# Context attention and projections of a batch's two chunks in one pass, with q, k, v loaded once

## The reference, cut to what matters

```python
# layer 0: 16 heads of 64 over 64 context rows, bias fside added twice
qh, kh, vh = heads(x @ wq + bq), heads(ctx @ wk + bk), heads(ctx @ wv + bv)
w = softmax(qh / 8 @ kh.T + fside + fside)
x = layernorm((w @ vh) @ wo + bo + x, eps=1e-6) * ln_g + ln_b            # the outer norm
# layer 1, 16 heads of 32
h1 = layernorm(x, eps=1e-5) * ln1_g + ln1_b                              # the inner norm
x = attention(h1, h1, quantised q, k, v, weights) @ wo + bo + x          # over all 1024 rows of the batch
h2 = layernorm(x) ...; x = attention(h2, ctx) @ wo + bo + x
h3 = layernorm(x) ...; a, g = split(h3 @ ff_w1 + b1)
x = (a * gelu(g)) @ ff_w2 + b2 + x
```

## Time and profile before

| | |
|---|---|
| median of 3 runs | 3404.15 us (3402.14 to 3405.04) |
| profiled execution, span | 3406.4 us |
| TensorE busy | 2956.5 us, 87% |
| VectorE / ScalarE / GpSimd busy | 2099.8 / 1669.4 / 1772.2 us |
| stage A of batch 0, from the first transpose of x | 120.5 to 376.8 us |
| stage A of batches 1, 2, 3 | 913.3 to 1161.4, 1695.2 to 1944.3, 2477.3 to 2728.3 us |

### The profile page before, as it was taken

The page is one execution under the profiler, slowest core; times in us unless marked ns, Lnnn a source line. Parts: engine busy times, 40 slices in busy tenths (PEclk is TensorE's granted clock), DMA queues, the critical chain, the costliest instruction groups (busy, mean ns, idle before and its releaser), DMA issues.

```text
span 3406.4 us, 50798 instructions
## 1 busy us (share of the span) xinstructions
PE 2956.5 (87%) x19712; PEld 2148.8 (63%) x19712; DVE 2099.8 (62%) x3031; ACT 1669.4 (49%) x2690; POOL 1772.2 (52%) x1695
## 2 busy tenths in 40 slices
PE   7677686887899899799889899899988889889999
PEld 6555455556677657566667656656777646656777
DVE  4556585773666586685565586676565577677521
ACT  5332572873333475574333375475333276386321
POOL 3554573884545274575355185475365176376321
PEclk9888657898999899899999999899999989999999
DMA  8753103334443213324353313323353322232444
GB/s 276 220 200 133 56 1 133 108 119 179 162 164 141 91 63 125 130 88 155 130 176 111 123 51 141 126 74 135 133 188 99 142 75 100 97 120 75 171 152 160
DMA packets 199758, 436.40 MB, mean 128 GB/s; under 512 B 94944, under 2 KB 103392, under 8 KB 182368
## 3 DMA queue, kind: packets, MB, share of 16 engines
q1 hardware_dynamic: 199520, 433.15, 36.1%
HBM read 363.38 MB, written 65.54 MB: 126 GB/s over the span
## 4 chain that ended last, share of the span: by engine, by line
PE 60%; DVE 11%; POOL 11%; ACT 7%; issue 6%; DMA 2%; SPq 1%; POOLq 0%; DVEq 0%; ACTq 0%
PE psum L1724 17%; PE psum L1726 15%; PE psum L1725 15%; PE psum L2020 5%; POOL w1b L998 3%; PE psum L2008 3%; DVE mx L1612 2%; ACT e L1302 2%; PE psum L2034 2%; ACT psum L1189 1%; DVE w1T L1624 1%; POOL u_lo L1017 1%; POOL rec L993 1%; DMA fw_lo<-pieces 1%; POOL w_lo L901 1%
## 5 line engine op out<-in xcount | busy, mean ns | idle before, releaser
L1612 DVE TENSOR_REDUCE mx<-psum 128x1 f32<-128x1024 f32 x512 | 623.1, 1218 | 121.2 <-PE psum L2009 121.0
L998 POOL TENSOR_SCALAR w1b<-e,rec 128x1024 f16<-128x1024 f32 x512 | 574.7, 1122 | 138.6 <-PE psum L2020 66.3
L1302 ACT ACTIVATE e<-psum,nb,scale 128x1024 f32<-128x1024 f32 x512 | 617.5, 1206 | 19.8 <-POOL w1b L998 3.1
L1724 PE MATMUL psum<-h_hi,fw_hi 128*128 128x512 f32 x1024 | 464.9, 454 | 30.9 <-DVE h_lo L1388 10.0
L1624 DVE TENSOR_SCALAR w1T<-psum 128x1024 bf16<-128x1024 f16 x512 | 352.0, 687 | 176.4 <-PE psum L2020 163.6
L1725 PE MATMUL psum<-h_lo,fw_hi 128*128 128x512 f32 x1024 | 415.8, 406 | 0.0
L1726 PE MATMUL psum<-h_hi,fw_lo 128*128 128x512 f32 x1024 | 415.2, 405 | 0.0
L2020 PEld LDWEIGHTS psum<-ident,w1b 128*128 128x128 f16 x4096 | 260.7, 105 | 207.7 <-issue 127.7
L2020 PE MATMUL psum<-ident,w1b 128*128 128x128 f16 x4096 | 354.3, 236 | 40.2 <-DVE w1T L1624 21.1
L907 POOL TENSOR_TENSOR rstd<-ve,mhalf 128x1 f32<-128x1 f32 x128 | 86.8, 678 | 484.8 <-DVE ve L1494 484.8
L1724 PEld LDWEIGHTS psum<-h_hi,fw_hi 128*128 128x128 f32 x1024 | 199.6, 195 | 152.4 <-issue 99.4
(11 more groups left out here) (181 smaller groups left out, 6237.0 us busy)
## 6 DMA issues: line engine op xcount, KB each, us to landing
fw_hi<-pieces SPq DMA_DIRECT2D x168, 512.0 KB, 3.3
fw_lo<-pieces SPq DMA_DIRECT2D x168, 512.0 KB, 4.4
w_hi<-kept SPq DMA_DIRECT2D x45, 1024.0 KB, 4.9
w_lo<-kept SPq DMA_DIRECT2D x45, 1024.0 KB, 7.4
mixed<-mixed SPq DMA_DIRECT2D x32, 1024.0 KB, 5.4
fbias<-in_fside_Bx16xSxS SPq DMA_DIRECT2D x64, 256.0 KB, 3.2
unsplit<-in_L_xattn_ff_w SPq DMA_DIRECT2D x24, 512.0 KB, 5.1
pieces<-fw_hi SPq DMA_DIRECT2D x24, 512.0 KB, 2.7
```

Source lines behind the costliest of these rows:

```text
L998: pool.tensor_scalar(w1b[u % NH][:], e1[u % NE][:], rec1[:, u % 8:u % 8 + 1], HALF, ALU.mult, ALU.add).then_inc(w1_ready.sem, 1)
L1302: act.activation(e1[s % NE][:], psum[:, i:i + 2, :].rearrange("p i n -> p (i n)"), ACT.Exp, bias=nb1[:, s % 4:s % 4 + 1], scale=scale[:, 0:1],
L1612: dve.tensor_reduce(mx1[:, s % 4:s % 4 + 1], psum[:, i:i + 2, :].rearrange("p i n -> p (i n)"), AX, ALU.max).then_inc(maxed1.sem, 1)
L1724: pe.matmul(o, s_hi, m_hi, start=first, stop=False)
```

## The change

- `cross(n)` of two chunks becomes `cross_pair(b)`: 22 steps s (11 of each chunk, `PAIR`), 12 products q, k, v of the first chunk, 12 of the second.
- The tail is taken apart. `LN_AT` puts the pieces "add", "outer" and "inner" of each tile at steps: those of the first chunk at steps 8 to 15, beside the second chunk's first products; those of the second at steps 19 to 26, beside the first chunk's q, k, v. The transposes of the second chunk's x and of the first's h1 are at steps 8 to 10 and 19 to 21 (`TURNED_AT`), those of the second's h1 before the first's last product.
- q1, k1 and v1 are loaded once a batch.
- The 16 hosted feed-forward steps lie at other slots (`IN_A`, quarters by slot; slot s+1 is the end of step s).
- The even chunk's z is a buffer of its own. Banks are given anew. The splits of blocks and the three prepared blocks of batch 0 lie at other steps.

```diff
+CROSS = STEPS0 + 3
+PAIR = NC * CROSS
+GROUPS_QKV = 12
+A_SLOTS = 2 * GROUPS_QKV + PAIR + 3
...
-FROM_A = host_quarters(8, 18, (0, 1, 2, 3, 4, 6, 10, 11, 12, 13, 15, 17, 19, 21))
+IN_A = [(0, 8), (1, 2), (2, 2), *((s, 4) for s in range(CROSS - 2, CROSS + 4)), (PAIR - 2, 4), (PAIR - 1, 4), (PAIR, 8),
+        (PAIR + GROUPS_QKV, 4), (PAIR + GROUPS_QKV + 1, 8)]
...
+LN_AT = {CROSS - 3: [("add", 0, 0)], CROSS - 2: [("add", 0, 1), ("outer", 0, 0)], CROSS - 1: [("add", 0, 2), ("inner", 0, 0), ("outer", 0, 1)],
+         CROSS: [("add", 0, 3), ("inner", 0, 1)], CROSS + 1: [("outer", 0, 2)], CROSS + 2: [("inner", 0, 2)],
+         CROSS + 3: [("outer", 0, 3)], CROSS + 4: [("inner", 0, 3)],
+         PAIR - 3: [("add", 1, 0)], PAIR - 2: [("add", 1, 1), ("outer", 1, 0)], PAIR - 1: [("add", 1, 2), ("outer", 1, 1)],
+         PAIR: [("add", 1, 3), ("inner", 1, 0)], PAIR + 1: [("inner", 1, 1), ("outer", 1, 2)], PAIR + 2: [("outer", 1, 3)],
+         PAIR + 3: [("inner", 1, 2)], PAIR + 4: [("inner", 1, 3)]}
+TURNED_AT = {CROSS - 3: (0,), CROSS - 2: (1,), CROSS - 1: (2, 3)}
...
-        first = [(NC * b + c, name) for c in range(NC) for name in ("M0", "N0", "M1", "N1", "q1", "k1", "v1")]
+        first = [(NC * b + c, name) for c in range(NC) for name in MIXED] + [(NC * b, name) for name in ("q1", "k1", "v1")]
...
+        (z0,) = scope([("z0", [P, NT, D], F32)])
```

SyncE's list:

```diff
+                    if c == 1 and i == 6:
+                        load_block((n, "q1"))
+                    if c == 1 and i == 7:
+                        load_block((n, "k1"))
+                    if c == 1 and i == 10:
+                        load_block((n, "v1"))
+                    if b == 0 and s == 10:
+                        keep_prep("o1")
+                        load_prep("q2")
+                    if b == 0 and s == 17:
+                        keep_prep("q2")
+                        load_prep("o2")
+                    host(1 + s)
+                if b == 0:
+                    for key in FIRST:
+                        keep_block(key)
+                    keep_prep("o2")
```

GpSimd's:

```diff
+                lows = {(0, 0): "N0", (0, 2): "M1", (0, 5): "N1", (0, 9): "M0", (1, 0): "N0", (1, 2): "M1", (1, 5): "N1"}
+                for s in range(PAIR):
+                    c, i = divmod(s, CROSS)
+                    n = first + c
                     m = i - 2
-                    if m >= 0:
+                    if 0 <= m < STEPS0:
                         pool.wait_ge(sum0_ready.sem, sum0_ready.at((n, m)))
                         pool.sem_inc(waits_over, 1)
                         e = e0[m % 4][:]
                         r = rr[m % 2][:, 0:8].rearrange("p (g o) -> p g o", o=1).broadcast_to((P, 8, SC))
                         pool.tensor_tensor(e, e, r, ALU.mult).then_inc(p0_ready.sem, 1)
...
+                    for half in range(2):
+                        name = lows.get((c, i - half))
+                        if name is not None:
+                            block_low((second if name == "M0" else n, name), range(2 * half, 2 * half + 2))
...
+                    if c == 0 and STEPS0 <= i:
+                        add_crow(second, i - STEPS0)
+                    norms(s)
+                    if b == 0:
+                        if s == 8:
+                            prep_low("o1")
+                        if s == 15:
+                            prep_low("q2")
+                        if s == 20:
+                            block_low((0, "q1"), range(4))
+                        if s == 21:
+                            block_low((0, "k1"), range(4))
+                    host(1 + s)
+                for g in range(GROUPS_QKV):
+                    norms(PAIR + g)
+                    if b == 0 and g == 3:
+                        block_low((0, "v1"), range(4))
+                    if b == 0 and g == 5:
+                        prep_low("o2")
+                    host(PAIR + 1 + g)
```

```diff
-                block_high((n, "N0"))
-                for i in range(STEPS0 + 2):
-                    if i == 1:
-                        block_high((n, "M1"))
-                    if i == 5:
-                        block_high((n, "N1"))
+                highs = {(0, 1): "M1", (0, 5): "N1", (0, 9): "M0", (1, 0): "N0", (1, 2): "M1", (1, 5): "N1"}
+                for s in range(PAIR):
+                    c, i = divmod(s, CROSS)
+                    n = first + c
+                    for k in TURNED_AT.get(i, ()):
+                        (x_high if c == 0 else h1_high)(second if c == 0 else first, k)
                     if i < STEPS0:
                         act.wait_ge(s0_ready.sem, s0_ready.at((n, i)))
                         act.activation(e0[i % 4][:], e0[i % 4][:], ACT.Exp).then_inc(e0_done.sem, 1)
...
                         act.activation(p0_hi[m % 2][:], bank(1), ACT.Copy).then_inc(phi_done.sem, 1)
+                    name = highs.get((c, i))
+                    if name is not None:
+                        block_high((second if name == "M0" else n, name))
...
+                    host(1 + s)
```

VectorE's step and end, and TensorE's end:

```diff
-                    host(1 + i)
-                host(A_TAIL - 1)
-                dve.wait_ge(bias_added.sem, bias_added.at(("bo", n)))
-                for t in range(NT):
-                    host(A_TAIL + t)
-                    residual_variance("o0", 0, n, t, EPS0)
+                    add_rows(s)
+                    for k in TURNED_AT.get(i, ()):
+                        (x_low if c == 0 else h1_low)(second if c == 0 else first, k)
+                    norms(s)
+                    host(1 + s)
...
+                for k in range(KT):
+                    h1_low(second, k)
+                host(PAIR + 1 + GROUPS_QKV)
...
+                for g in range(GROUPS_QKV):
+                    if g == GROUPS_QKV - 1:
+                        for k in range(KT):
+                            h1_T(second, k)
+                    project(first, g)
+                    host(PAIR + 1 + g)
+                host(PAIR + 1 + GROUPS_QKV)
+                for g in range(GROUPS_QKV):
+                    project(second, g)
+                    host(PAIR + 2 + GROUPS_QKV + g)
+                host(A_SLOTS - 1)
```

More of the change, by code:

```diff
@@ L74, in host_quarters @@
     ends = []
[L75 to L78, removed]
+    for s in range(A_SLOTS if in_A else 0):
+        ends.append(sum(quarters for first, quarters in in_A if first <= s))
+    first, start = ends[-1] if ends else 0, len(ends)
     for s in range(S_SLOTS):
@@ L203, in bank_fills @@
     for b in range(B):
-        for n in range(NC * b, NC * b + NC):
-            fills += [("xT", n, k, 2 + k) for k in range(KT)]
+        first, second = NC * b, NC * b + 1
+        for n in (first, second):
+            fills += [("xT", n, k, 2 + k if n == first else (0, 2, 3, 0)[k]) for k in range(KT)]
             for i in range(STEPS0):
@@ L437, in build @@
         batches = [range(NC * b, NC * b + NC) for b in range(B)]
-        norms = [(j, n, t) for ns in batches for part in ((0, 1), (2, 3)) for n in ns
-                 for js in ((part,) if part[0] == 0 else ((2,), (3,))) for t in range(NT) for j in js]
+        norms = [key for ns in batches for keys in (
+            [(j, ns[c], t) for j, c, t in LN_NORMS], [(j, n, t) for n in ns for j in (2, 3) for t in range(NT)]) for key in keys]
         var_ready = signal("var_ready", norms)
@@ L766, in cross @@
                     load_block((0, "M1"))
[L767 to L778, removed]
+                load_x(second)
@@ L779, in cross @@
+                if b == 0:
                     for key in FIRST:
                         keep_block(key)
[L781 to L795, removed]
-                    for v in (8, 9):
-                        load_piece(NC * b - 1, v)
@@ L798, in cross @@
[L798 to L803, removed]
+                    keep_prep("o2")
+                for g in range(GROUPS_QKV + 1):
+                    host(PAIR + 1 + g)
+                if b > 0:
+                    wait_filled(sp, ("q1", second, 3))
+                    for v in (8, 9):
+                        load_piece(n - 1, v)
@@ L1529, in feed, with cross_pair, x_low @@
                         residual(key, xs(n, m))
-            def cross(n):
+            def cross_pair(b):
+                first, second = NC * b, NC * b + 1
                 def host(s):
-                    if n >= NC:
-                        feed(NC * (n // NC) - 1, FROM_A, A_SLOTS * (n % NC) + s)
-                host(0)
-                for k in range(KT):
+                    if b > 0:
+                        feed(first - 1, FROM_A, s)
+                def x_low(n, k):
                     key = ("xT", n, k)
@@ new lines, in cross_pair @@
+                for g, (kind, m) in enumerate(QKV):
+                    add_rows(PAIR + g)
+                    norms(PAIR + g)
+                    to_integers(first, kind, m)
+                    host(PAIR + 1 + g)
+                for k in range(KT):
+                    h1_low(second, k)
```

(6 more changed lines are left out.)

307 lines of the change are left out of this document (175 added, 132 removed).

## The result

The changed kernel takes 3430.81 us (median of 4 runs, 3429.11 to 3434.24), against 3404.6 for the kernel before beside it: a ratio of 1.0081, 95% interval 1.0066 to 1.0095. It is 26 us slower. The prediction said 3383 (3355 to 3402) and gave a slower kernel 9 in 100, so it was wrong in sign and in range.

A forecast was written before the change was run, and what follows sets the result against it. TensorE's list was taken to bound stage A, so only its waits could go: batch 0 gains 24 us, three later batches lose about 1 us each, 21 us in all, giving 3383 us (3355 to 3402).

The forecast's parts named there:

- the second item under "Batches 1 to 3": Later batches, first chunk: TensorE waits 1.6 us for GpSimd's scaled weights, as in the kernel before.
- steps 11 to 15: Batches 1 to 3, second chunk's start: GpSimd's late chain makes TensorE wait 8.4 us, taken as 11 for stretched VectorE.
- The clock: Batch 0's stage A: TensorE's clock rises once the old tails go, gaining 0 to 5 us, taken as 3.
- gate copy at slot 1: Batches 1 to 3: hosted step waits 3.6 us for bank 6, emptied by ScalarE's copy behind the first s0's exponential.
- piece 7: Batches 1 to 3, slot 22: piece issued behind v1's block, so step 12 waits 5.5 us.
- last hosted step: Batches 1 to 3, second chunk's h1: 2.2 us wait for bank 7, which VectorE empties behind four low parts.
- scaled weights and step 8: Batches 1 to 3: scaling waits of 1.6 us in the first chunk and 0.7 in each chunk at step 8.
- Batch 0: Its stage A: waits fall from 71.7 to 50.8 us; with 3 us from a higher clock it gains 24 us.
- The slower one: VectorE, GpSimd, TensorE chain late in steps 9 to 16; batch 0 gains 15, later batches lose 8; 3413 us, chance 0.09.
- The first rival: Later batches gain 6 us each, with VectorE unstretched and GpSimd's high parts earlier; 3362 us, chance 0.3.
- No change: Waits only move, in batch 0 as well, bound by GpSimd's prepared blocks and VectorE; within 7 us of 3404, chance 0.08.
- the upper bound: Steps 10 to 15 of later batches: VectorE stretched beside GpSimd's long operations adds about 5 us of waits.

The follow-up runs named there:

- n1_early: Changed kernel with only N1's high part put back ahead of step 5's exponential on ScalarE: 3394.38 us, ratio 0.9977 to the kernel before.
- before_n1late: Kernel before, with only N1's high part at step 5 moved behind the exponential and p_hi copy: 3452.11 us, ratio 1.0137.
- experiment 6: Changed kernel with the high parts of N1, M1 and second-chunk N0 ahead of the exponential, plus three repairs of hosted-step and transfer order: 3348.7 us, ratio 0.9835.
- norms_late: Changed kernel with outer and inner norms of the first chunk's tiles 2 and 3 three steps later: 3433.45 us, ratio 1.0091.
- queue3: Changed kernel with hosted half steps one slot later, v1's block behind piece 7, last hosted step's bank emptied before second-chunk h1: 3402.06 us, ratio 0.9996.
- slots_only: Changed kernel with only the hosted feed-forward half steps of slots 1 and 2 moved to slots 2 and 3: 3413.47 us, ratio 1.0025.

## Why the prediction was wrong

**The step that failed** is the second item under "Batches 1 to 3": "Scaled weights, first chunk: 1.6 us as now". I wrote out step 11 to 15 with ScalarE's list, and there noted that N0's and M1's high parts now stand behind an exponential and a copy. N1's moved in the same way, from `if i == 5` ahead of the exponential to the end of the step, and I took its step over from the old trace. The row of the old scaling waits was still right (1.8 us measured at step 3); a new wait of 4.1 us stood beside it, at step 6 of seven of the eight chunks, and one of 1.2 us in the eighth. n1_early shows its size in the changed kernel, 36 us, and before_n1late shows that it needs nothing else of the change. Without this one misplacement the kernel would have been 0.2% faster than before, inside the predicted range, with half of the forecast gain or less.

In all, the four stages A are 28 us longer, and the sums said 21 shorter. Of these 49 us, 30 are the new waits (5.3 in batch 0, 8.3 in each of the others) and 22 are TensorE's busy time (8.4 in batch 0, where it rose by 5.4 and I had it fall by 3, and 13.4 in the others together, where I had nothing). The waits on the list came out 3 us better than said.

**The clock** is the second term that failed. I gave it 3 us of gain in batch 0 and nothing elsewhere. In batches 1 to 3 its mean over the stage fell from 0.97 or 0.98 to 0.93 and 0.94, and TensorE's busy time rose by 3.4 to 5.8 us a batch. The clock has two levels, 1.2 and 2.4 GHz (0.50 and 1.00), and the trace shows it fall at the new waits. Behind the first 4.14 us wait of batch 2, in the changed kernel, as a window and in TensorE's timeline:

```profile
1753.00:1757.00 4.00, 3.97 (x12) 3.30 (x13) 3.20 (x5) 1.12 (x2) 4.00 (x3) 0.50 0.29 66
```

```profile
1758.21 0.63 PE L1819 MATMUL psum<-w_lo,p_hi 128*128 128x512 f32 x1
1758.64 0.59 PE L1820 MATMUL psum<-w_hi,p_lo 128*128 128x512 f32 x1
...
1759.31 0.40 PE L1819 MATMUL psum<-w_lo,ht_hi 128*128 128x512 f32 x1
1759.54 0.40 PE L1820 MATMUL psum<-w_hi,ht_lo 128*128 128x512 f32 x1
```

The twelve matmuls of the product behind the wait start 0.43 us apart, the next ones 0.23. That product takes 5.3 us (1753.80 to 1759.06) instead of 2.7. One program at two clocks gives the price too. Stages A of batches 2 and 3 of the repaired kernel of experiment 6 have the same work, and 19.5 and 19.2 us without TensorE busy; at 0.96 it is busy 220.5 us, at 0.98 217.8:

```profile
2430.00:2667.00 237.00, 217.76 (x996) 177.10 (x993) 140.16 (x256) 84.84 (x112) 104.30 (x85) 0.98 0.36 124
```

TensorE's busy time in batch 2 was 226.4 us with the longest waits, 223.4 and 224.8 with the high parts moved, 223.2 and 223.4 with the order mended, 220.5 with both. So it went with the waits, though not in strict order. The mean clock alone does not give it either: the kernel before had 222.2 us at 0.98. One wait of 4.1 us cost 5.9 us in the old kernel (47 over 8).

**Batches 1 to 3, the other waits**, were right in place and nearly in size:
- gate copy at slot 1: 3.6 said, 3.54 measured;
- steps 11 to 15: 8.4 by the lists, 11 taken; 6.25 + 1.71 + 1.89 = 9.85 measured;
- piece 7: 5.5 said, 5.75 measured;
- last hosted step: 2.2 said, 2.08 measured;
- scaled weights and step 8: 1.6 + 1.4 said, 1.81 + 1.43 measured.

They sum to 24.5 us against 25.3 said. With 2 x 4.14 this is 32.7, and the waits that I left out on both sides make the rest. The 0.15 us for a restart was too small a price for a long wait: the product behind the 4.14 us one took 2.5 us more than at the upper level. The list was a good tool, and it was one instruction short. It was also not the floor that I took it for: I called the gate's and the piece's waits the change's price, and three small edits of order took 29 us off.

**Batch 0** gained 14.8 us, not 24. The sum of the waits was nearly right there, and the clock's term had the wrong sign. By the tables TensorE is without work 72.7 us before and 51.3 after, which is 21 us less, as said; but it is busy 189.7 us instead of 184.3, where I had 3 us less. The mean clock misled me: it rose, from 0.86 to 0.90, because the long stretches at the lower level in which TensorE stood idle went, such as the 16.8 us at the end. In their place came shorter ones with matmuls in them. That the waits met their sum is partly luck: 5.3 us are N1's (4.12 and 1.20), and those on the list came to 4 us less than said. With N1's high part back the stage is 234.2 us, 22.1 less than before. The page had the items: the 16.8 us at the end became 1.7, the scaling wait behind o1's low part is 6.07 us (7.0 said, 6.3 of it the block), q1's low part 6.36 (5.8 said), and h1 of the second chunk 3.6 (4.9 said):

```profile
PE psum L2074 <- POOL e L998: 29.6, 11, 6.1
...
PE psum L1818 <- POOL w_lo L939: 6.4, 1, 6.4
PE psum L1818 <- DVE ht_lo L1452: 5.3, 4, 3.0
```

**The rivals.** The slower one ended on the right side with the wrong mechanism. It put the loss into outer norms stretched beside GpSimd, and asked 17 us of wait in steps 9 to 16; the scaling had 9.9 there. Its 15 us of gain in batch 0 was met (14.8) by luck, since it came about otherwise. norms_late took these pieces away from the start of the second chunk and nothing came back. The first rival, a gain in every batch, came true only in the repaired kernel (3348.7 against its 3362), and partly for a reason that it did not have, the order of the transfers. "No change" fails too: the waits of batch 0 did go.

**The rule of the Trainium skill** (GPSIMD Engine Reference, section Specifications), that GpSimd's work contends with VectorE's instructions of two SBUF inputs, is borne out. The outer norm's instruction by line, changed kernel (minimum, median, maximum in ns), and both instructions of the outer norm in VectorE's timeline, the second with the GpSimd low parts that it stands beside:

```profile
L1626 DVE SCALAR_TENSOR_TENSOR x<-x,mv,row_L_xattn_ln_g x32: 743/748/1775, 201.9 to 2686.1; 128x512 f32<-128x512 f32 x32
L1653 DVE TENSOR_TENSOR e<-e,row_max x64: 691/794/1636, 140.0 to 2645.0; 128x512 f32<-128x512 f32 x64
```

```profile
1784.39 1.77 DVE L1626 SCALAR_TENSOR_TENSOR x<-x,mv,row_L_xattn_ln_g 128x512 f32<-128x512 f32 x1
...
1799.32 1.65 DVE L1628 SCALAR_TENSOR_TENSOR x<-x,rstd,row_L_xattn_ln_b 128x512 f32<-128x512 f32 x1
```

```profile
1798.70 3.40 POOL L939 TENSOR_TENSOR w_lo<-mixed,w_hi 128x512 fp32r<-128x512 f32 x2
```

In the kernel before no outer norm took over 0.753 us; now the longest takes 1.775. The sum with the bias (L1646), which reads one tensor from SBUF and one from PSUM, stays between 0.672 and 0.690 us all through the changed kernel. But the softmax difference gained what the outer norm lost, with a median of 0.794 us instead of 1.290, and VectorE's busy time in stage A of batch 2 is 139.8 us against 141.0. The rule holds, and VectorE's total did not grow by it: the contention goes to whatever stands beside GpSimd. So the stage did not take the upper bound that I had worked out from it: the waits of steps 11 to 15 were 9.85 us, nearer to the 8.4 of the unstretched lists than to the 13.4 of the stretched ones.

## What to carry to other kernels

When a list of one in-order engine is written anew, put every instruction of it beside the old one, those of the steps that seem untouched too, and ask of each what it now stands behind. An instruction that needs nothing of the step (the split of a prefetched block) belongs ahead of the engine's wait, never behind it: one such line, 1.9 us long, cost 36 us here, because another in-order engine and then TensorE queued behind it.

Before a restructuring is judged, its small orders have to be put right one at a time. The same pairing is 0.8% slower or 1.65% faster than the kernel before, by the place of a few lines.

## What the hardware showed that I had not expected

A wait of some 4 us costs more than itself. In the old kernel eight added waits of 4.14 us, 33 us, made it 47 us slower, and in three of its stages the difference stands as longer TensorE busy time at a lower mean clock (0.86 to 0.84, 0.98 to 0.96, 0.98 to 0.97). The changed kernel ran its later stages A at 0.93 to 0.94 where the old one had 0.97 to 0.98, with the same matmuls. And a mean clock over a stage can rise while TensorE gets slower, as in batch 0: it counts the idle stretches too.

The order of two transfers is worth 2 us each time. With v1's block issued 2.7 us ahead of piece 7, TensorE waited 5.75 us for the piece; with the block behind it, 3.5 us. SyncE's issues in the changed kernel, and in queue3:

```profile
1868.45 0.32 SPq L671 DMA_DIRECT2D w_hi<-kept  x1
...
1871.17 0.32 SPq L704 DMA_DIRECT2D fw_hi<-pieces  x1
```

```profile
1848.02 0.32 SPq L704 DMA_DIRECT2D fw_hi<-pieces  x1
...
1848.86 0.43 SPq L671 DMA_DIRECT2D w_hi<-kept  x1
```

The piece's wait ended 7.1 us after its first issue in the changed kernel (at 1878.26), and 4.8 us after it in queue3 (at 1852.82). slots_only, which leaves this order as it is, still waits 5.7 us.
